# Heads of a stack laid out group-first instead of head-first in SBUF, in a two-branch attention kernel (16 × 256 × 128, float32)

## What is computed

```python
xn = _layernorm(x)
x = x + encoder(xn) + expert(xn)
# encoder: 4 layers, causal attention of 16 heads of 8 features, with a linear position bias (ALiBi)
for i in range(4):
    x = x + mha(layer_norm(x, ...), mask, ...)           # scores / sqrt(8) + mask, softmax, times v
    x = x + gelu(layer_norm(x, ...) @ ffn1.T + b) @ ffn2.T + b
# expert: 1 layer, full attention of 8 heads of 16 features, feature widths 128, 64, 32, 16 by quarter of tokens
```

## Time and profile before

| | us, if nothing else is said |
|---|---|
| three executions | 1640.9, 1649.48, 1649.96 |
| median | 1649.48 |
| the profiled execution | 1640.9 |
| its span (first to last instruction) | 1639.1 |
| PE busy | 1421.8 (87%) |
| ACT busy | 1223.2 (75%) |
| DVE busy | 1131.8 (69%) |
| POOL busy | 614.3 (37%) |
| DMA, mean share of 16 engines (SP's queue; POOL's queue) | 33.3%; 8.3% |
| DMA packets, all; under 2 KB | 104789; 70728 |

### The profile page before, as it was taken

How to read it: one execution, slowest core, us unless ns; L and a number is a source line. 1 busy time by engine, 2 the same in 40 slices (tenths; PEclk the granted TensorE clock), 3 DMA queues, 4 the chain that set the end, 5 groups by cost and what they waited for, 6 DMA issues and landing times.

```text
span 1639.1 us, 38563 instructions
## 1 busy us (share of the span) xinstructions
PE 1421.8 (87%) x10720; PEld 946.2 (58%) x10720; DVE 1131.8 (69%) x2851; ACT 1223.2 (75%) x2165; POOL 614.3 (37%) x1052
## 2 busy tenths in 40 slices
PE   0677787568999999999999999999999989999995
PEld 0445554335666666666666666666666656666653
DVE  6567676347777777677677766777776767777762
ACT  3233333238999898898999888999888988888884
POOL 5232222123333343333333333334333345555443
PEclk9999888779999999999999999999999999999997
DMA  3332333045444444444444445444444444444430
GB/s 107 100 114 89 107 92 101 24 122 149 121 124 127 117 116 126 134 129 119 120 129 119 122 121 133 129 119 121 127 119 123 129 128 125 124 125 125 123 90 10
DMA packets 104789, 187.60 MB, mean 114 GB/s; under 512 B 19912, under 2 KB 70728, under 8 KB 104720
## 3 DMA queue, kind: packets, MB, share of 16 engines
q1 hardware_dynamic: 89904, 150.45, 33.3%
q0 software_dynamic: 14848, 36.72, 8.3%
HBM read 120.87 MB, written 65.01 MB: 113 GB/s over the span
## 4 chain that ended last, share of the span: by engine, by line
PE 53%; DVE 17%; issue 14%; DMA 9%; POOL 2%; DVEq 1%; ACT 1%; SPq 1%; POOLq 0%; ACTq 0%
PE pvp L979 11%; PE exp_ps L956 7%; DVE negm L698 6%; PE mxp L923 6%; PE dense L1009 6%; PE dense L1018 5%; PE dense L868 5%; DMA blocks<-split_L 4%; PE mxp L927 4%; DVE xn L666 3%; PE dense L896 2%; PE dense L997 2%; DVE ost L744 2%; PE mxp L868 2%; DMA blocks<-negt 2%
## 5 line engine op out<-in xcount | busy, mean ns | idle before, releaser
L831 ACT ACTIVATE probs<-exp_ps 128x512 f32<-128x512 f32 x896 | 525.0, 593 | 289.1 <-PE exp_ps L956 286.4
L698 DVE TENSOR_REDUCE negm<-mxp 128x2 f32<-128x512 f32 x896 | 569.2, 683 | 90.3 <-PE mxp L927 72.6
L956 PE MATMUL exp_ps<-qbd_l,kst_l 128*128 128x512 f32 x768 | 368.5, 495 | 8.3 <-issue 4.3
L923 PE MATMUL mxp<-blocks,qst 104*128 104x512 f32 x768 | 325.5, 453 | 34.5 <-DMA blocks<-split_L 19.7
L855 ACT ACTIVATE exp_ps<-masktf 128x512 f32<-128x512 f32 x513 | 308.8, 602 | 22.6 <-DVE rest L766 6.5
L927 PE MATMUL mxp<-maskb,identb 128*128 128x256 bf16 (+1 forms) x768 | 247.6, 322 | 0.0
L498 POOL TENSOR_SCALAR veps<-mv 128x2 f32<-128x2 f32 x144 | 31.7, 220 | 560.9 <-DVE mv L657 557.2
L923 PEld LDWEIGHTS mxp<-blocks,qst 104*128 104x128 f32 x768 | 149.0, 194 | 84.2 <-DVE negm L698 37.0
L979 PE MATMUL pvp<-probs,vst_l 128*32 128x256 f32 (+1 forms) x4096 | 194.5, 330 | 0.6 <-ACT probs L831 0.6
L744 DVE COPY ost<-pvp 128x512 f32<-128x512 f32 x80 | 55.3, 692 | 201.6 <-PE pvp L979 201.6
L956 PEld LDWEIGHTS exp_ps<-qbd_l,kst_l 128*128 128x128 f32 x768 | 144.4, 195 | 40.8 <-issue 31.3
(11 more groups left out here) (95 smaller groups left out, 2006.6 us busy)
## 6 DMA issues: line engine op xcount, KB each, us to landing
split_L<-hi SPq DMA_DIRECT2D x256, 128.0 KB, 2.1
qst<-split_L SPq DMA_DIRECT2D x64, 384.0 KB
kst_l<-split_L SPq DMA_DIRECT2D x64, 384.0 KB
qbd_l<-split_L SPq DMA_DIRECT2D x256, 96.0 KB
split_L<-lo POOLq DMA_DIRECT2D x128, 128.0 KB, 2.1
blocks<-split_L SPq DMA_DIRECT2D x128, 96.0 KB
blocks<-split_L POOLq DMA_DIRECT2D x128, 96.0 KB, 4.4
split_F<-hi SPq DMA_DIRECT2D x64, 128.0 KB, 2.1
```

Source lines behind the costliest of these rows:

```text
L698: dve.tensor_reduce(heads[:, g, first:first + count], mxp[:, (plan.max_chunks * g + ch) % 3, :].rearrange("p (h t) -> p h t", h=count), AX ...
L831: act.activation(probs[:, g[0], ch, :], exp_ps[:, (plan.exp_chunks * g[0] + ch) % 2, :], ACT.Exp, scale=plan.scale).then_inc(q.b_exp, 1)
L923: pe.matmul(mxp[:, bank, :], qst[0:BIAS_END, g[0], qt * P:(qt + 1) * P], kbd[0:BIAS_END, first:first + count, g[0], 0:keys], start=True, s ...
L956: pe.matmul(exp_ps[:, bank, :], kst[plan.name][:, s, g[0], kt * P:(kt + 1) * P], rhs, start=not on_diagonal, stop=True, skip_group_check=T ...
```

## The change

The order of the head columns is turned round: head i of group g stands at g·4 + i (expert: g·2 + i), so that the heads of one group stand together. The view `queries` goes, and slices of `qbd` take its place. Everything that writes or reads the block-diagonal operands follows, and so do `negm` and the constant rows. Bytes, number of DMAs, waits and the order of all engines stay; what changes is how each access walks through a partition.

```diff
@@ -239,8 +239,7 @@
         blocks = sb("blocks", [P, 2 * EXPERT.heads, T], F32R)
         qbd = {"L": sb("qbd_l", [P, 2, ENCODER.heads, T], F32R),
                "F": blocks.rearrange("p (s h) t -> p s h t", s=2)}
-        kbd = blocks.rearrange("p (i g) t -> p i g t", g=GROUPS)
-        queries = {name: stack.rearrange("p s (i g) t -> p s i g t", g=GROUPS) for name, stack in qbd.items()}
+        kbd = blocks.rearrange("p (g i) t -> p g i t", g=GROUPS)
         qst = sb("qst", [P, GROUPS, T], F32R)
         kst = {"L": sb("kst_l", [P, 2, GROUPS, T], F32R), "F": sb("kst_f", [P, 2, GROUPS, T], F32R)}
         probs = sb("probs", [P, GROUPS, 3, 512])
@@ -359,7 +358,7 @@
                 sp.dma_start(qst[0:plan.hg * rows, :, :].bitcast(F32),
                              sc[0].rearrange("i c d (g t) -> (i c d) g t", t=T)).then_inc(q.max_stk[s], 16)
                 for i in range(plan.hg // 2):
-                    sp.dma_start(kbd[i * rows:(i + 1) * rows, i, :, :].bitcast(F32),
+                    sp.dma_start(kbd[i * rows:(i + 1) * rows, :, i, :].bitcast(F32),
                                  sc[1, i].rearrange("c d (g t) -> (c d) g t", t=T)).then_inc(q.max_stk[s], 16)
 
             def stack_queries_and_keys(plan, q, u, r, s):
@@ -374,9 +373,9 @@
                 settle(sp, passed_sp)
                 sp.dma_start(kst[plan.name][0:plan.hg * rows, s, :, :].bitcast(F32),
                              sc[1].rearrange("i c d (g t) -> (i c d) g t", t=T)).then_inc(q.stk[s], 16)
-                qd = queries[plan.name][:, s].bitcast(F32)
+                qd = qbd[plan.name][:, s].bitcast(F32).rearrange("p (g i) t -> p g i t", g=GROUPS)
                 for i in range(plan.hg if plan.causal else plan.hg // 2):
-                    sp.dma_start(qd[i * rows:(i + 1) * rows, i, :, :],
+                    sp.dma_start(qd[i * rows:(i + 1) * rows, :, i, :],
                                  sc[0, i].rearrange("c d (g t) -> (c d) g t", t=T)).then_inc(q.stk[s], 16)
 
             def share(plan, q, step, u, s, r):
@@ -406,7 +405,7 @@
             sp.wait_ge(s_rounded, 6)
             for i in range(ENCODER.hg):
                 rows = slice(ALIBI_ROW + 2 * i, ALIBI_ROW + 2 * i + 2)
-                sp.dma_start(kbd[rows, i, :, :].bitcast(F32), kst["L"][rows, 0, :, :].bitcast(F32)).then_inc(s_bias, 16)
+                sp.dma_start(kbd[rows, :, i, :].bitcast(F32), kst["L"][rows, 0, :, :].bitcast(F32)).then_inc(s_bias, 16)
             sp.wait_ge(q.wa, 16)
 
             def load_a(layer):
@@ -555,10 +554,10 @@
                         else:
                             wait_past(pool, q.b_s, plan.exp_chunks * GROUPS * (u - 1))
                             settle(pool, passed_pool)
-                            side, to = 0, queries["F"][:, s].bitcast(F32)
+                            side, to = 0, qbd["F"][:, s].bitcast(F32).rearrange("p (g i) t -> p g i t", g=GROUPS)
                         rows = COPIES * plan.dh
                         for i in range(plan.hg // 2, plan.hg):
-                            pool.dma_start(to[i * rows:(i + 1) * rows, i, :, :],
+                            pool.dma_start(to[i * rows:(i + 1) * rows, :, i, :],
                                            split[plan.name][s][side, i].rearrange("c d (g t) -> (c d) g t", t=T))\
                                 .then_inc(q.pool_stk[s], 16)
                     elif step == "op":
@@ -694,8 +693,8 @@
                 dve.wait_ge(q.b_max, c + 1)
                 if g == 0 and ch == 0:
                     wait_past(dve, q.b_nt, u - 1)
-                heads = negm[:, s, qt, 0:plan.heads].rearrange("p (i g) -> p g i", g=GROUPS)
-                dve.tensor_reduce(heads[:, g, first:first + count],
+                h0 = plan.hg * g + first
+                dve.tensor_reduce(negm[:, s, qt, h0:h0 + count],
                                   mxp[:, (plan.max_chunks * g + ch) % 3, :].rearrange("p (h t) -> p h t", h=count),
                                   AX.X, ALU.max, negate=True).then_inc(q.b_red, 1)
 
@@ -921,7 +920,7 @@
                         if plan.causal:
                             keys = 512 // count
                             pe.matmul(mxp[:, bank, :], qst[0:BIAS_END, g[0], qt * P:(qt + 1) * P],
-                                      kbd[0:BIAS_END, first:first + count, g[0], 0:keys], start=True, stop=True,
+                                      kbd[0:BIAS_END, g[0], first:first + count, 0:keys], start=True, stop=True,
                                       skip_group_check=True)
                             o = mxp[:, bank, :].rearrange("p (h t) -> p h t", h=count)[:, :, qt * P:(qt + 1) * P]
                             last = pe.matmul(o, identb[:, :], maskb[:, 0:count, :], start=False, stop=True,
@@ -929,7 +928,7 @@
                         else:
                             for k in range(count):
                                 last = pe.matmul(mxp[:, bank, k * T:(k + 1) * T],
-                                                 queries["F"][0:MAX_ROW, s, k, g[0], qt * P:(qt + 1) * P],
+                                                 qbd["F"][0:MAX_ROW, s, plan.hg * g[0] + k, qt * P:(qt + 1) * P],
                                                  kst["F"][0:MAX_ROW, s, g[0], :],
                                                  start=(k == 0), stop=True, skip_group_check=True)
                         last.then_inc(q.b_max, 1)
@@ -938,7 +937,7 @@
                         dense_job(1, q.b_negt, 1, off)
                         transposes(dense[1], [negm[:, s, t, 0:plan.heads] for t in range(NT)], q.b_nt)
                     elif step == "exp":
-                        ch = g[1]
+                        ch, h0 = g[1], plan.hg * g[0]
                         if g == [0, 0]:
                             if plan.causal:
                                 pe.wait_ge(q.stk[s], 16 * plan.stack_dmas * (r + 1))
@@ -947,10 +946,10 @@
 
                         wait_past(pe, q.b_exp, plan.exp_chunks * (GROUPS * u + g[0]) + ch - 1)
                         if not plan.causal:
-                            kt, rhs, on_diagonal = ch, queries["F"][:, s, :, g[0], :], False
+                            kt, rhs, on_diagonal = ch, qbd["F"][:, s, h0:h0 + 2, :], False
                         else:
                             kt, qt = BLOCKS[ch]
-                            rhs, on_diagonal = queries["L"][:, s, :, g[0], qt * P:(qt + 1) * P], kt == qt
+                            rhs, on_diagonal = qbd["L"][:, s, h0:h0 + 4, qt * P:(qt + 1) * P], kt == qt
                         if on_diagonal:
                             pe.wait_ge(q.b_seed, 2 * (GROUPS * u + g[0]) + kt + 1)
                         pe.matmul(exp_ps[:, bank, :], kst[plan.name][:, s, g[0], kt * P:(kt + 1) * P], rhs,
@@ -1053,11 +1052,11 @@
     high = (bias.view(np.uint32) & np.uint32(0xFFFFF000)).view(np.float32)
     low = bias - high
     n = P - ALIBI_ROW
-    rq = np.zeros((n, ENCODER.hg, GROUPS, T), np.float32)
+    rq = np.zeros((n, GROUPS, ENCODER.hg, T), np.float32)
     rk = np.zeros((n, GROUPS, T), np.float32)
     for i in range(ENCODER.hg):
         for part, b in enumerate((high, low)):
-            rq[2 * i + part, i, :, :] = 1.0
+            rq[2 * i + part, :, i, :] = 1.0
             rk[2 * i + part] = b[i::ENCODER.hg]
     rk[n - 1] = 1.0
     rkf = np.zeros((n, GROUPS, T), np.float32)
```

## The result

| | before | changed |
|---|---|---|
| median | 1649.44 us (6 runs) | 1657.73 us (6 runs) |
| lowest to highest | 1640.9 to 1652.61 | 1656.75 to 1661.21 |
| ratio to before, 95% interval | 1 | 1.0065 (1.0044 to 1.0086) |
| span of the profiled execution | 1639.1 us | 1654.3 us |

The changed kernel is slower by 0.65%, some 11 us by the ratio and 8.3 us between the medians (the ratio is not taken from the two medians, so the two differ). The interval lies above 1, but the difference is smaller than the 1% that was set as clear. The forecast was 1656.5 us. The two profiled spans lie 15 us apart, mainly because the profiled execution of before was its fastest.

What follows compares the result with a forecast made beforehand. PE in its written order was taken to set the pace, with transfers sometimes ahead. Key pieces 6 us plus expert branch 1, all else 0, made 7 us on the 1649.48 us median: 1656.5 us, own range 1643 to 1666.

Steps and rivals of the forecast that it cites:

- The place: Encoder units, PE's first max matmul: keys land in blocks about when PE needs them, so later landing is paid nearly in full.
- The key loads' pieces: Encoder key loads: 1 KB pieces cost 28 ns per row, partly hidden by congestion; 0.10 us per unit, 6 us in all.
- port rule: Congested half of the key transfer: 8 ports carry 218 GB/s; if they limit, pieces are free there and 6 us becomes 3.
- The issue of those loads: Encoder key loads: SP's issue 0 to 0.22 us longer per DMA, hidden behind the qst load; cost taken as 0.
- the loads land late in every unit: Slower rival, before each unit's first max matmul: issue 0.44 and engine time 0.17 us unhidden; 1675 us, chance 0.37.
- The query loads: Encoder query loads (L379): longer transfer and issue covered, since they serve the next slot's exp steps; cost 0.
- PE's reading: Exp and max matmuls: moving operand's columns closer together or contiguous; gain taken as 0, with 19 us as the bound.
- DVE's writes: DVE's reductions into negm: contiguous instead of every fourth element; at most some 3 us of engine time, taken as zero.
- The rival of faster reading: Faster rival, PE's matmuls and key waits: contiguous runs give back 19 us, finer pieces 12.1; 1618 us, chance 0.10.
- that of no effect: Rival on the transfers: the queue moves a row's 4 pieces as one, so nothing changes; 1649.5 us, chance 0.05.
- The expert branch: Expert branch loads, 16 units: at most 2.7 us, most units have cover; taken as 1 us.
- The signs: Profile after: about 49,000 more small packets, blocks wait 5 to 10 us longer, L361 370 to 600 ns, DMA share slightly up.

Runs made afterwards that it cites:

- keys_only: Kernel before with only the keys for the maxima (kbd) laid out group-first, queries, negm and constant rows left head-first; ratio to before 1.0096.
- queries_only: Changed kernel with kbd put back head-first, so only queries (encoder and expert branch), negm and constant rows are group-first; ratio to before 0.9996.
- the delays: Kernel before with SP held up by 6 or 12 semaphore increments ahead of each key load, transfers untouched; ratios to before 0.9990 and 1.0022.

## Why the prediction was right or wrong, point by point

*The place* was right. The max matmul's wait for the keys is where the time is lost: the chain's DMA share grew, keys_only has the whole loss and queries_only none.

*The key loads' pieces* were undersized. The step that failed is "there the engines stand waiting for something else, and 7 ns per KB should vanish in it". In the congested half a busy engine moves 13.8 GB/s after 15.6 (means of 62 units), and by keys_only the term is not 0.10 us per unit but about 0.2, the full price of 0.17 or a little more. The price itself, 28 ns per row, came from comparing stores with loads, so the direction of the transfer stood in it as well as the size of the pieces. It gave sizes close to the loss at 2 and 4 runs and too much from 4 to 8, and the engines' time in queries_only contradicts it; that it came out so near is in part luck.

The reading that I hung on the Trainium skill's port rule ("SBUF — State Buffer", "Door 1: The DMA port swizzle"), that a port limit would make the pieces free in that half, is not borne out: the key loads' pieces cost 0.36 to 1.47%. Whether a limit is at work stays open. In the unit of the earlier trace rows the rate of 197 GB/s fell to 181, but the mean of 62 units was 173 GB/s before and 172 after, and no row shows ports.

*The issue of those loads* was out of its bounds in size and right in effect. I bounded it by the `hi` store at 0.22 us per DMA on SP and got 0.43, since the nearest row with a third dimension had another shape (32 × 4 × 256, 596 ns) than the loads (24 × 4 × 256, 807 ns). But the step that takes the issue as hidden held in the main: the delays put this term between nothing and 0.2%. The rival "the loads land late in every unit" put 0.44 us of its 0.61 on the issue. It named the right place and the wrong share, and its 1675 us was not reached.

*The query loads* cost nothing, as forecast, though SP's issue of them went from 365 to 758 ns. *PE's reading* and *DVE's writes* are zero as far as can be told: a max matmul of one run advances PE by 0.24 us, as one of two runs did, an exp matmul by 0.23 instead of 0.24, the reductions kept their 681 to 683 ns, and queries_only is not faster. Two rows of the chain after, the first a max matmul of one run:

```profile
886.87 0.24 PE mxp L922
888.13 0.23 PE exp_ps L955
```

The rival of faster reading is out, and so is that of no effect, by the interval and by the packets. *The expert branch* I priced at 1 us; queries_only includes it and shows no loss. PE and PEld waited 12.0 us for its loads after 8.9 before, so a few us may stand there that the intervals don't show.

*The sum*: by keys_only (15 us, of which 0 to 3 are issue) the pieces cost 12 to 15 us where I had 6. That the whole change measured 8 us between medians (11 by the ratio) and so came near to the forecast's 7 is luck as far as the largest term goes; the few us between keys_only and the whole change are within what the two intervals allow and have no cause shown.

*The signs.* The packets gave 40,000 and not 49,000, because POOL's queue moves four 1 KB pieces as one packet; the condition was stated. The wait for `blocks` grew by 6.8 us, within the 5 to 10 that I gave. SP's issue, 807 ns, lies outside my 370 to 600, and the DMA share did not rise by one or two hundredths but went from 33.3 to 33.1% on SP's queue and from 8.3 to 7.9% on POOL's. That miss, too, says that a price on every piece was wrong.

## What to carry to other kernels

Find out first which transfer the busiest engine waits for at the end of a race, here one of three groups of loads of the same size. Here a layout that cuts the rows into more runs cost on that transfer and was free on the others, even though SP's issue time doubled on all of them. Don't take finer pieces for free because the engines look congested: on the load at the end of the race they were not. A layout between the two extremes can win most of it back (2 runs cost a bit over a third of 4). A price that fits the measured loss still has to be held against the engines' own time. To price an issue, hold the queue up by itself; cutting a DMA in two to imitate it brings in another cost.

## What the runs showed of the hardware that was not expected

SP took 374 ns to issue a load of 24 rows × 1024 elements, 807 to 817 ns with 2, 4 or 8 runs per row, but 607 ns for 48 rows × 4 runs in the expert branch (419 ns as 48 × 1024). So in these shapes a third dimension costs SP 0.2 to 0.4 us, with 2, 4 or 8 runs alike, and the 24-row load, with half the pieces, costs more than the 48-row one. The rows of the changed kernel, tile `blocks`:

```profile
L378 SPq DMA_DIRECT2D blocks<-split_F x16: 581/607/718, 42.2 to 279.4; - x16
L560 POOL DMA_DIRECT2D blocks<-split_F x16: 612/620/627, 42.4 to 278.6; - x16
```

The query loads of the same shape, 24 rows × 4 runs, took 758 ns, so the tile or its place in the queue matters a little as well. POOL's issue hardly depends on the shape (542, 606, 614 and 652 ns at 1, 2, 4 and 8 runs). And the same bytes in two more DMAs per unit, 128 in the encoder, cost 1.03%, as much as four runs per row did.
